# One count per quarter: how TensorE waits for and releases four gathered tiles in a graph kernel's aggregation loops

## The reference, cut to what matters

```python
# layer 0, twice:            agg = segment_sum(norm[:, None] * x[src], dst)
# layer 1, there and back:   he_feat = segment_sum(x_prime[node_idx], he_idx)
#                            out     = segment_sum(he_feat[he_idx], node_idx)
# layer 2:                   light   = segment_sum(vals[:, None] * emb[cols], rows)
# layer 3:                   edge attention with a softmax over all edges
```

## Time and profile before

| | us |
|---|---|
| median of 3 runs (lowest to highest) | 8914.25 (8909.64 to 8922.52) |
| profiled execution, its own time | 9010.64 |
| span of that execution | 9008.9 |
| PE, DVE, ACT, POOL busy in the span | 4358.2, 3499.7, 1204.0, 5294.0 |
| gathers of `aggregate` (line 368): count, busy | 3696, 3689.6 |

### The profile page before, as it was taken

How to read it: one execution, slowest core, us unless ns; L and a number is a source line. 1 busy time by engine, 2 the same in 40 slices (tenths; PEclk the granted TensorE clock), 3 DMA queues, 4 the chain that set the end, 5 groups by cost and what they waited for, 6 DMA issues and landing times. The chain is left out here.

```text
span 9008.9 us, 102562 instructions
## 1 busy us (share of the span) xinstructions
PE 4358.2 (48%) x17220; PEld 3232.7 (36%) x17221; DVE 3499.7 (39%) x11515; ACT 1204.0 (13%) x4632; POOL 5294.0 (59%) x5326
## 2 busy tenths in 40 slices
PE   6555554555543333145555555543333335666665
PEld 3333332333333333123333333322223225656563
DVE  8444444223232222041112322243333355666666
ACT  0000000000000000020000000010000024444443
POOL 0566665777766666626666666646666625555551
PEclk9999996555555555565555555555555567888887
DMA  9111111111111111152111111121111123333332
GB/s 158 53 45 45 45 45 45 45 45 44 45 44 44 44 44 44 44 33 46 45 46 42 45 45 44 45 42 43 44 43 44 43 50 90 95 97 95 95 95 42
DMA packets 665641, 492.66 MB, mean 55 GB/s; under 512 B 515113, under 2 KB 565684, under 8 KB 665476
## 3 DMA queue, kind: packets, MB, share of 16 engines
q0 software_dynamic: 183232, 378.81, 15.6%
q1 hardware_dynamic: 482228, 112.18, 7.1%
q10 hardware_dynamic: 144, 1.28, 0.1%
HBM read 411.96 MB, written 79.95 MB: 55 GB/s over the span
## 5 line engine op out<-in xcount | busy, mean ns | idle before, releaser
L368 POOL DMA_INDIRECT gathered<-node_table,idx x3696 | 3689.6, 998 | 2223.1 <-issue 1098.7
L387 PE MATMUL ps<-onehots,gathered 128*128 128x128 f32 x4128 | 1631.4, 500 | 1508.9 <-DMA gathered<-node_table,idx 1359.1
L387 PEld LDWEIGHTS ps<-onehots,gathered 128*128 128x128 f32 x4128 | 1033.2, 312 | 2106.7 <-DMA gathered<-node_table,idx 1960.7
L389 PE MATMUL ps<-onehots,gathered 128*128 128x128 f32 x3264 | 1054.6, 469 | 1440.3 <-DVE agg L452 779.6
L389 PEld LDWEIGHTS ps<-onehots,gathered 128*128 128x128 f32 x3264 | 769.6, 320 | 1726.1 <-issue 980.8
L408 DVE TENSOR_TENSOR onehots<-iota,off_t 128x512 f32<-128x512 f32 x736 | 508.6, 692 | 2164.9 <-PE ps L387 1188.8
L921 POOL DMA_INDIRECT gathered<-node_table_xq,idx x832 | 793.8, 954 | 763.1 <-PE ps L1022 226.6
L611 POOL DMA_INDIRECT bucketed_edges<-edge_rows,idx x782 | 774.9, 991 | 424.6 <-issue 258.9
L452 DVE TENSOR_TENSOR agg<-agg,ps 128x128 f32 x1632 | 466.7, 286 | 757.6 <-issue 643.5
L660 PE MATMUL ps<-gathered 128*128 128x49 f32 x1568 | 346.4, 414 | 703.0 <-DVE gathered L645 492.8
L660 PEld LDWEIGHTS ps<-gathered 128*128 128x128 f32 x1568 | 338.3, 332 | 711.1 <-DVE gathered L645 497.5
(11 more groups left out here) (258 smaller groups left out, 4476.1 us busy)
## 6 DMA issues: line engine op xcount, KB each, us to landing
gathered<-node_table,idx POOLq DMA_INDIRECT x3696
bucketed_edges<-edge_rows SPq DMA_DIRECT2D x52, 544.0 KB
edge_rows<-bucketed_edges SPq DMA_DIRECT2D x208, 128.0 KB
edge_rows<-in_edge_attr_dram SPq DMA_DIRECT2D x192, 128.0 KB
gathered<-node_table_xq,idx POOLq DMA_INDIRECT x832
bucketed_edges<-edge_rows,idx POOLq DMA_INDIRECT x782
node_table<-t_nodes SPq DMA_DIRECT2D x3, 3136.0 KB
node_table<-x_nodes SPq DMA_DIRECT2D x1, 3136.0 KB
```

Source lines behind the costliest of these rows:

```text
L368: nc.gpsimd.indirect_dma_start(g[:, k, :], None, table, bass.IndirectOffsetOnAxis(m.idx[:, k:k + 1], 0)).then_inc(S["landed"][k], 16)
L387: nc.tensor.matmul(m.ps[:, q, 0:P], g[:, k, :], m.oh[:, k, :], start=e == 0, stop=e == G - 1).then_inc(S["used"], 1)
L389: nc.tensor.matmul(m.ps[:, q, e * P:(e + 1) * P], g[:, k, :], m.oh[:, k, :], start=True, stop=True).then_inc(S["used"], 1)
```

## The change

Three things are changed in `aggregate`. PE waits for all four `landed` semaphores of a quarter ahead of the quarter's first matmul, instead of for one ahead of each matmul. Only the fourth matmul of a quarter raises `used`. And all who wait for `used`, or start it off, count in quarters instead of in tiles: ACT, DVE in two places, and PE's own first increment. The matmuls, the gathers and the DVE work stay as they are.

```diff
@@ scalar
-                    act.wait_ge(S["used"], nt + G * q + G)
+                    act.wait_ge(S["used"], n * NQ + q + 1)
@@ tensor
-            pe.sem_inc(S["used"], U)
+            pe.sem_inc(S["used"], NQ)
@@
-                    pe.wait_ge(S["landed"][k], nt + 16)
+                    if e == 0:
+                        for j in range(k, k + G):
+                            pe.wait_ge(S["landed"][j], nt + 16)
                     if dst_order:
-                        nc.tensor.matmul(m.ps[:, q, 0:P], g[:, k, :], m.oh[:, k, :], start=e == 0, stop=e == G - 1).then_inc(S["used"], 1)
+                        last = nc.tensor.matmul(m.ps[:, q, 0:P], g[:, k, :], m.oh[:, k, :], start=e == 0, stop=e == G - 1)
                     else:
-                        nc.tensor.matmul(m.ps[:, q, e * P:(e + 1) * P], g[:, k, :], m.oh[:, k, :], start=True, stop=True).then_inc(S["used"], 1)
+                        last = nc.tensor.matmul(m.ps[:, q, e * P:(e + 1) * P], g[:, k, :], m.oh[:, k, :], start=True, stop=True)
+                    if e == G - 1:
+                        last.then_inc(S["used"], 1)
@@ vector, head
-                        v.wait_ge(S["used"], n * U + G * q + G)
+                        v.wait_ge(S["used"], n * NQ + q + 1)
@@ vector, body
-                    v.wait_ge(S["used"], nt + G * q + G + U)
+                    v.wait_ge(S["used"], n * NQ + q + 1 + NQ)
```

## The result

| | before | after |
|---|---|---|
| median, us (20 runs each) | 8921.15 | 8939.63 |
| lowest to highest, us | 8909.64 to 8936.1 | 8920.99 to 8959.74 |
| ratio of the times, 95% interval | | 1.0016 (1.0009 to 1.0023) |
| profiled execution, span | 9008.9 | 8928.3 |

The forecast was 8614 us. The changed kernel takes 8939.63: no gain, and a loss of 0.16% that is just large enough to be told from nothing. So the 80 us between the two spans are not what the change did (30 of them lie in hop2, 21 in bucket_edges, which the change doesn't touch), and I read the two traces for where POOL stops, not for their lengths.

The account below looks back on a forecast made before the run. POOL was taken to bound the kernel, with 637.5 us of stops within reach. -310 + 6 = -304 us profiled, times 0.989 -301, gave 8614 us from 8914; own range 8500 to 8750, 8 in 10 from 8380 to 8960.

Parts of the forecast that it names:

- What bounds the kernel: Whole kernel: POOL's gathers and issue gaps bound it; 637.5 us of stops, from held-back counts, are all the change can touch.
- One count for four: Five stages: a count takes 2.75 us to pass, so one per quarter keeps up with POOL; -310 us.
- Waits moved to the front: PE's waits at a quarter's head: free within the stream, 1.27 us at each of five stage ends, 6 us in all.
- The stop's end: Stops that stay: up to 1.27 us longer each, if PE's last matmuls release the held bunch.
- rival 4: Slower: every stop stays and ends after PE's later last matmul, +142 us, 9054 us; chance 0.19.
- Rival 3: Same: the hold depends on POOL's stream, draining DMAs end a stop, only 6 us left, 8920 us; chance 0.09.
- Light: Stage light: 20% of 208.8 us of waits go, -42 us, as DVE's 6.0 us quarter limits next.
- The clock: PE in the stages: if pauses between bursts bring the half clock forward, the assumed 2.07 us burst already includes it.

Follow-up runs that it names:

- one_count_3: Before with only the fourth matmul of a quarter counting, PE's waits left one per matmul, on a chip with stops: 8937.49 us (before there 8926.02).
- before_again: The kernel before, unchanged, profiled again on a chip without stops: 7899.13 us (before there 7903.49).
- fill_copy: After with three tensor_scalar instructions of 784 columns per iteration added on DVE in hyperedges, chip without stops: 7998.69 us (before there 7907.74).
- one_count: Before with only the fourth matmul of a quarter counting, PE's waits left one per matmul, chip without stops: 7902.81 us, ratio to before 1.0000.
- one_count_2: The same kernel as one_count, against before on another chip without stops: 7897.76 us, ratio 1.0000.
- before_third: The kernel before, unchanged, profiled on a further chip without stops: 7898.76 us (before there 7897.81).
- after_third: The changed kernel, unchanged, on a chip with stops: 8935.27 us, ratio to before 1.0007.

## Why the prediction was wrong, point by point

- **What bounds the kernel.** Right: POOL, its issue gaps and 637.5 us of stops. Right too, that the counts are held and not PE's work. But these stops were taken as a trait of the kernel. The same kernel has none on three other chips, and no row of one trace could tell that. The count of 179 also holds gaps of 0.3 us; 171 are over 0.6.
- **One count for four: the step that failed.** It read the 11.0 us of the earlier trace rows as four times 2.75 us, the price of passing one count. Nothing in the rows said that counts pass one by one. In after a single count was held 15.3 us in the same stage, and one_count_3 kept 155 of 179 waits with a quarter of the counts. What the runs show in its place is a hold that goes with POOL's stream, whatever is waiting in it: it ends mostly when POOL stops (76 of the 116 late copies of hop1 before, 73 of 106 after), and for the rest while POOL streams, as in the earlier trace rows at 343.68. What makes it is open. The row that spoke against the step was known: bucket_edges, with one count for eight matmuls and a hold of 23.4 us. It was taken for the lower bound of the gain only, and should have been given more weight. Expected -310 us, measured none.
- **Waits moved to the front: 6 us.** About right in size, in part by luck: +10.0 us between two undisturbed traces, of which 5.8 outside the stages, but only 1.2 of them at a stage's end where they recur. The other 4.2 were not foreseen: the moved waits shift DVE's matrix instruction against the gathers, +12.3 us in hop2 and -15.7 in members. The text took "nothing" for the three waits at the head of a quarter, which holds only for PE.
- **The stop's end.** In the earlier trace rows the bunch left 2.4 us after PE's last matmul, and rival 4 made PE the one who releases it, 1.27 us later at 107 stops. In after PE's burst ends 0.18 us ahead of the copy and the stop is no longer. In hop1, hyperedges and members the first copy of a stop comes 5.0, 5.5 and 5.0 us after POOL's last gather's start before (medians), and 4.6, 4.9 and 4.7 after, while in hop1 PE's last matmul moved from 2.2 to 0.2 us ahead of it. So in before the stop's end isn't set by PE's last matmul; in after the two come so close that it might be. In members alone the stops grew, from 4.6 to 5.2 us in the mean, and were fewer, 33 for 36; the stage kept its length (1195.3 and 1195.6 us). Rival 4's +142 us did not come.
- **The rivals.** Rival 3 ("same") named it right, hold by stream, burst hidden at the stop's end, 6 us left, 8920 us; that the DMAs' draining ends a stop, as it had it, no run shows. It had a chance of 0.09 against 0.50 for a price that no row showed.
- **Light.** Expected -42 us; 208.8 went to 185.8. Once again no more than the pair differs elsewhere: stages without a changed line (bucket_edges, attend) were 21 and 14 us shorter in the profiled after. That DVE was next in line, with a quarter of 6.0 us of its own, was a misreading, and so was laying its gaps of 3.10 and 1.10 us to the port that `tensor_scalar` shares with POOL. Where POOL doesn't stop, it streams without a pause, and light of before_again shows the same four matrices back to back in 1.2 us (start, us, instruction):

```profile
6030.41 1.21 DVE L413 TENSOR_SCALAR onehots<-iota,off_t,ew_t 128x128 f32<-128x128 f32 x4 [2.24 <-PE ps L389]
```

The gaps belong to what is slow on a chip with stops.
- **The clock.** Right that it would cost nothing: bursts took 2.08 us for the 2.07 assumed, and 2.07 also at the full level in hop1 of fill_copy. But the half clock in hop1 of after is not shown to come from the pauses between bursts: it comes and goes from one execution to the next. Of after's 20 executions 5 had a mean granted clock of 0.56, as the profiled one, and 14 one of 0.77 to 0.78, and one_count and one_count_2, the same kernel, show either level in the first two stages:

```profile
PEclk9999999999999999996555555555555556999997
...
PEclk5555555555555555556555555555555556999997
```

## What to carry to other kernels

Before a wait is priced per event, look in the trace for a place where the number of events differs already; here one stood in the rows and had the answer. When the bounding engine streams and stops, look at its pace over a whole stage: time taken out of the stream can come back as stops, as 147 us of shorter gathers did as 144 us of waits. Before a loss is laid to the kernel, profile it on a second chip. And an instruction of another engine that reads two operands from SBUF while POOL issues gathers is worth removing where nothing else holds the stream: 1.5% here, far more than the 0.1% that the change cost.

## What the runs showed of the hardware

- The same kernel takes 8920 us on one or two chips and 7900 on three others, and much of the difference is in the waiting: PE's counts reach ACT within 0.14 us on the latter (before_third, hop1), up to 17.7 us late on the former while POOL issues indirect DMAs, one count as four. DVE's own queue instructions are slow there too, up to 0.88 us in hop1 of after for 0.13.
- A DVE instruction with two SBUF inputs over the start of a gather mostly makes it longer, 1.23 to 1.33 us in the mean of a stage instead of 0.94; four `tensor_scalar` in its place leave it at 0.95.
- Code added to one stage went with a slower later one: instruction packets went from 27 to 147, and attend got 63 to 80 us longer.
- PE at half clock for all five stages cost nothing measurable: the executions of after_third at a mean granted clock of 0.56 have a median of 8935.4 us, those at 0.78 one of 8935.3.
